# Expert routing in three groups of token tiles instead of two, with two of the three sigmoids moved into the state-space loop

## The reference

```python
x = x + _L1_attn_ref(_L1_cond_ref(x, ...), ...)        # state-space model
x = x + _L1_ffn_ref(_L1_cond2_ref(x, ...), ...)        # gate, then experts

def _L1_ffn_ref(hidden_states, w_gate, w1, w2, w3):
    x = hidden_states.reshape(-1, D)
    router_logits = x @ w_gate.T
    routing_weights = jax.nn.softmax(router_logits.astype(jnp.float32), axis=-1)
    routing_weights, selected_experts = jax.lax.top_k(routing_weights, TOP_K)
    routing_weights = routing_weights / jnp.sum(routing_weights, axis=-1, keepdims=True)
    out = jnp.zeros_like(x)
    for e in range(NUM_EXPERTS):
        expert_weight = jnp.sum(routing_weights * (selected_experts == e), axis=-1, keepdims=True)
        h = jax.nn.silu(x @ w1[e].T) * (x @ w3[e].T)
        out = out + h @ w2[e].T * expert_weight
    return out.reshape(B, S, D)
```

## Time and profile before

| what | value |
| --- | --- |
| median of three executions (lowest, highest) | 700.4 us (700.04, 701.31) |
| span of the profiled execution, first to last instruction | 698.6 us |
| busy PE, PEld, DVE, ACT, POOL | 537.6, 392.4, 405.1, 370.2, 147.6 us |
| chain that ended last, by engine | PE 52%, DVE 31%, ACT 9%, issue 4%, DMA 2% |
| mean granted clock of TensorE | 0.910 of full speed |
| weight fetches of the experts | 23 x 1408 KB and 23 x 768 KB |

### The profile page before, as it was taken

How to read it: one execution, slowest core, us unless ns; L and a number is a source line. 1 busy time by engine, 2 the same in 40 slices (tenths; PEclk the granted TensorE clock), 3 DMA queues, 4 the chain that set the end, 5 groups by cost and what they waited for, 6 DMA issues and landing times.

```text
span 698.6 us, 13906 instructions
## 1 busy us (share of the span) xinstructions
PE 537.6 (77%) x5666; PEld 392.4 (56%) x5668; DVE 405.1 (58%) x597; ACT 370.2 (53%) x791; POOL 147.6 (21%) x115
## 2 busy tenths in 40 slices
PE   0095778677587855579998999979539999999980
PEld 0053555555455722454655666648529999997570
DVE  5889999989996578946835445543541111211223
ACT  6986789968877238645566455562312222222212
POOL 1000000000001138702068455220021222222210
PEclk9997699998878999899999999998659999999996
DMA  9500000000001000000000000000159999988825
GB/s 351 180 1 1 1 1 1 2 1 1 1 1 32 1 0 1 2 0 1 2 3 2 3 2 2 2 2 3 61 206 421 421 419 354 335 332 314 327 110 188
DMA packets 18479, 71.38 MB, mean 102 GB/s; under 512 B 4848, under 2 KB 9968, under 8 KB 14704
## 3 DMA queue, kind: packets, MB, share of 16 engines
q1 hardware_dynamic: 15408, 64.20, 24.2%
q0 software_dynamic: 1920, 5.25, 2.0%
q10 hardware_dynamic: 1088, 1.05, 0.4%
HBM read 65.77 MB, written 4.72 MB: 101 GB/s over the span
## 4 chain that ended last, share of the span: by engine, by line
PE 52%; DVE 31%; ACT 9%; issue 4%; DMA 2%; POOL 1%; SPq 0%; ACTq 0%; DVEq 0%; POOLq 0%
PE PS L1412 40%; DVE arena L933 4%; DVE nmx L1020 4%; DVE arena L930 4%; PE PS L1918 2%; PE PS L1987 2%; PE PS L1694 1%; DVE arena L945 1%; DVE arena L944 1%; DVE R L947 1%; DVE A L952 1%; DVE arena L939 1%; DVE arena L940 1%; PE PS L1559 1%; ACT arena L767 1%
## 5 line engine op out<-in xcount | busy, mean ns | idle before, releaser
L1412 PE MATMUL PS<-arena 128*128 128x128 f32 (+5 forms) x1374 | 156.6, 295 | 17.7 <-DVE arena L1117 11.6
L1412 PEld LDWEIGHTS PS<-arena 128*128 128x128 f32 (+4 forms) x1376 | 125.7, 164 | 41.1 <-issue 24.5
L611 ACT ACTIVATE arena<-PS,nmx 128x128 f32<-128x128 f32 (+1 forms) x128 | 52.2, 423 | 34.7 <-DVE nmx L1020 34.7
L1360 DVE TENSOR_TENSOR R<-arena,PS 128x128 f32<-128x128 f32 x16 | 4.6, 288 | 88.8 <-ACT arena L861 88.8
L1476 PE MATMUL PS<-arena 32*128 32x128 f32 (+1 forms) x128 | 22.9, 439 | 34.0 <-ACT arena L611 33.8
L389 POOL TENSOR_SCALAR arena<-ident,gcol 128x128 f32<-128x128 f32 x4 | 2.4, 605 | 220.2 <-DMA gcol<-in_gcol 220.2
L449 POOL TENSOR_TENSOR arena<-arena 128x1024 f32<-128x1024 f32 x16 | 37.8, 2369 | 42.9 <-DVE arena L1199 34.8
L481 POOL DMA_INDIRECT ypair<-arena,oid x20 | 19.8, 988 | 122.1 <-ACT arena L867 122.1
L1412 PE MATMUL PS<-arena,R 128*128 128x256 f32 x192 | 44.2, 380 | 0.6 <-ACT arena L867 0.6
L1412 PEld LDWEIGHTS PS<-arena,R 128*128 128x128 f32 x192 | 35.2, 190 | 5.1 <-issue 1.0
L933 DVE TENSOR_TENSOR_SCAN arena<-dmat,arena 128x1023 f32<-128x1023 f32 x16 | 37.6, 2348 | 0.6
(11 more groups left out here) (302 smaller groups left out, 1205.3 us busy)
## 6 DMA issues: line engine op xcount, KB each, us to landing
arena<-in_moe SPq DMA_DIRECT2D x23, 1408.0 KB, 7.8
arena<-in_moe SPq DMA_DIRECT2D x23, 768.0 KB, 9.6
inproj<-in_inproj SPq DMA_DIRECT2D x1, 1344.0 KB, 10.5
arena<-in_fT SPq DMA_DIRECT2D x1, 1024.0 KB, 5.0
xT<-in_xT SPq DMA_DIRECT2D x1, 1024.0 KB, 5.4
R<-in_w1T SPq DMA_DIRECT2D x1, 1024.0 KB, 7.5
R<-in_w2T SPq DMA_DIRECT2D x1, 1024.0 KB, 9.5
R<-in_w3T SPq DMA_DIRECT2D x1, 1024.0 KB, 11.6
```

The source lines that it names most:

```text
L611: sc.activation(pr[u % 2][:, j, 0:n], PS[:, 2 * (u % 2) + j // 2, (j % 2) * 256:(j % 2) * 256 + n], ACT.Exp, bias=nmx[:, u % 2, j:j + 1], ...
L1412: last = mm(dst, l, r, start=(n == 0), stop=(n == len(pairs) - 1))
```

## The change

The eight tiles are routed in groups of four, two and two (`ROUTE`), with PSUM banks 0, 1 and 3 for a group's logits and ranks. The sigmoid of group 0 moves from behind `inverse_root(5)` to ahead of it, the sigmoid of group 1 is new in ScalarE's iteration 7, ahead of `turned(6)`, and the sigmoid of group 2 stands after the loop, now ahead of the first copy of token rows. VectorE and TensorE take the groups in the order 1, 0, 2.

```diff
 ROUTE = ((0, 4), (4, 6), (6, 8))          # new; ROUTE_BANK = (0, 1, 3)
@@ ScalarE
+            def sigmoid_tiles(g):
+                lo, hi = ROUTE[g]
+                act.wait_ge(S["dve_x"], X_FFN + hi)
+                sc.activation(A[:, :, lo * P:hi * P], xT[:, :, lo * P:hi * P], ACT.Sigmoid).then_inc(S["act_sg"], 1)
...
                 if i + 1 < NT:
                     by_chunk(i + 1)
+                else:
+                    sigmoid_tiles(1)
+                    sc.preload_act_table_set(LN_EXP)
                 if i:
                     turned(i - 1)
+                    if i == NT - 2:
+                        sigmoid_tiles(0)
+                        sc.preload_act_table_set(LN_EXP)
                     inverse_root(i - 1)
-                if i == NT - 2:
-                    sigmoid_x(3, 0)
-                    sc.preload_act_table_set(LN_EXP)
...
+            sigmoid_tiles(2)
             token_rows(0)
-            sigmoid_x(3, 1)
             token_rows(1)
@@ VectorE
-            gate(3, 0)
+            gate_tiles(0)
+            gate_tiles(1)
             gated(NT - 1)
             add_out(NT - 2)
...
+            top_values(1)
+            top_two(1)
             top_values(0)
             top_two(0)
             add_out(NT - 1)
-            gate(3, 1)
-            top_values(1)
-            top_two(1)
             places(0)
+            gate_tiles(2)
+            place_rows(0)
+            places(1)
+            top_values(2)
+            top_two(2)
+            place_rows(1)
             blocks()
-            places(1)
+            places(2)
+            place_rows(2)
             tokens_of_blocks()
@@ TensorE
+            logits(1)
+            turn(NT - 1)
             logits(0)
-            turn(NT - 1)
+            output(NT - 1)
             token_rows(0)
-            output(NT - 1)
             ranks(0)
-            logits(1)
-            pe.wait_ge(S["dve_x"], X_SSD)
+            ranks(1)
+            logits(2)
             token_rows(1)
-            ranks(1)
+            ranks(2)
             pe.wait_ge(S["act_atok"], 1)
             token_x(0)
```

More of the change, by code:

```diff
@@ L830, in _ @@
             token_x(1)
-            act.wait_ge(S["dve_mask"], 2)
+            act.wait_ge(S["dve_mask"], 3)
             sc.activation(wt[:, 0, :], delta[:], ACT.Sigmoid)
@@ L1251, in _, with gate_tiles, top_values, top_two @@
                     front(i + 1)
-            gate(3, 0)
+            def gate_tiles(g):
+                lo, hi = ROUTE[g]
+                dve.wait_ge(S["act_sg"], 7 + g)
+                a_ = A[:, :, lo * P:hi * P]
+                r_ = R[:, 3, lo // 4].rearrange("p (a n) -> p a n", a=CT)[:, :, lo % 4 * P:((hi - 1) % 4 + 1) * P]
+                done(v.tensor_tensor(a_, a_, r_, ALU.mult), "dve_A")
+            gate_tiles(0)
+            gate_tiles(1)
             gated(NT - 1)
             add_out(NT - 2)
[L1256 to L1263, removed]
+            def top_values(g):
+                lo, hi = ROUTE[g]
+                dve.wait_ge(S["pe_lg"], (6, 2, 8)[g])
+                done(v.tensor_copy(lg[:, lo:hi, :], PS[:, ROUTE_BANK[g], NE * lo:NE * hi].rearrange("p (i e) -> p i e", e=NE)))
+                for i in range(lo, hi):
                     done(v.max(top[:, i, :], lg[:, i, :]))
-            def top_two(c):
-                h = slice(4 * c, 4 * c + 4)
-                for i in range(4 * c, 4 * c + 4):
+            def top_two(g):
+                lo, hi = ROUTE[g]
+                h, b48 = slice(lo, hi), [P, hi - lo, NE]
+                for i in range(lo, hi):
                     done(v.max_index(tix[:, i, :], top[:, i, :], lg[:, i, :]))
@@ L1276, in top_two, with places @@
                 done(v.tensor_tensor(mb[:, h, :], oh[:, 0, h, :], oh[:, 1, h, :], ALU.add), "dve_mask")
-            def places(c):
-                h = slice(4 * c, 4 * c + 4)
+            def places(g):
+                lo, hi = ROUTE[g]
+                h = slice(lo, hi)
                 dve.wait_ge(ld["route"], 7 * 16)
-                dve.wait_ge(S["pe_rank"], 2 * c + 1)
+                dve.wait_ge(S["pe_rank"], (1, 2, 4)[g])
                 for s in range(2):
-                    done(v.tensor_tensor(pick[:, s, h, :], bank(c, 4 * NE).rearrange("p (i e) -> p i e", i=4), oh[:, s, h, :], ALU.mult))
+                    done(v.tensor_tensor(pick[:, s, h, :], PS[:, ROUTE_BANK[g], NE * lo:NE * hi].rearrange("p (i e) -> p i e", e=NE), oh[:, s, h, :],
+                                         ALU.mult))
                 done(v.tensor_reduce(rnk[:, :, h], pick[:, :, h, :], X, ALU.add))
@@ L1288, in places, with place_rows @@
                 done(v.scalar_tensor_tensor(pos[:, :, h], quo[:, :, h], -float(UNIT), rnk[:, :, h], ALU.mult, ALU.add))
-                four = [P, 4, UNIT]
+            def place_rows(g):
+                lo, hi = ROUTE[g]
+                h, some = slice(lo, hi), [P, hi - lo, UNIT]
                 for s in range(2):
-                    done(v.tensor_tensor(posoh[:, s, h, :], iop[:].unsqueeze(1).broadcast_to(four),
-                                         pos[:, s, h].unsqueeze(2).broadcast_to(four), ALU.is_equal))
+                    done(v.tensor_tensor(posoh[:, s, h, :], iop[:].unsqueeze(1).broadcast_to(some),
+                                         pos[:, s, h].unsqueeze(2).broadcast_to(some), ALU.is_equal))
             def blocks():
                 full, odd = fullodd[:, 0, :], fullodd[:, 1, :]
-                dve.wait_ge(S["pe_rank"], 2)
+                dve.wait_ge(S["pe_rank"], 3)
                 done(v.tensor_scalar(nunit[:], bank(2, NE), 1.0 / UNIT, 31.5 / UNIT, ALU.mult, ALU.add))
@@ L1831, in _, with logits @@
                     output(i - 1)
[L1834 to L1837, removed]
+            def logits(g):
+                pe.wait_ge(S["dve_A"], 7 + g)
+                for i in range(*ROUTE[g]):
+                    acc(PS[:, ROUTE_BANK[g], i * NE:(i + 1) * NE], [(A[:, kt, i * P:(i + 1) * P], wgate[:, kt, :]) for kt in range(CT)], "pe_lg")
             def token_rows(c):
@@ L1845, in token_rows, with ranks @@
                 last.then_inc(S["pe_at"], 1)
-            def ranks(c):
-                pe.wait_ge(S["dve_mask"], c + 1)
-                if c:
+            def ranks(g):
+                pe.wait_ge(S["dve_mask"], (2, 2, 3)[g])
+                if g == 2:
                     acc(bank(2, NE), [(oneb[:], mb[:, k, :]) for k in range(NT)], "pe_rank")
[L1852 to L1855, removed]
+                for i in range(*ROUTE[g]):
+                    for k in range(i + 1):
+                        last = mm(PS[:, ROUTE_BANK[g], i * NE:(i + 1) * NE], ub[:] if k == i else oneb[:], mb[:, k, :], start=(k == 0), stop=(k == i))
                 last.then_inc(S["pe_rank"], 1)
@@ L2013 @@
 ROWS_BANK = (2, 5)
+ROUTE = ((0, 4), (4, 6), (6, 8))
+ROUTE_BANK = (0, 1, 3)
 X_ATT = NT
```

## The result

| | before | after |
| --- | --- | --- |
| median of the timed executions, 4 each (lowest, highest) | 700.39 us (700.04, 701.31) | 689.66 us (689.18, 691.69) |
| span of the profiled execution | 698.6 us | 687.9 us |
| mean granted clock of TensorE | 0.910 | 0.905 |

The change makes the kernel faster: ratio 0.986, 95% interval 0.9839 to 0.9882. Forecast were 689.4 us, and 11.0 us of gain in the span; it is 10.7.

The account below looks back on a forecast made before the run. Routing bounds when the fixed 90 us expert stage starts: 4.9 us earlier at the last addition, plus VectorE's 18.55 us instead of 24.62 to `gid`, give 11.0 us: span 687.6, with 1.8 timed offset 689.4 us, range 687.0 to 692.6.

Parts of the forecast that it names:

- A: First sigmoid moves into ScalarE's gap in iteration 6: TensorE's 2.97 us wait goes, tile 7's VectorE work starts 5.76 us earlier.
- B: Second sigmoid queued ahead of tile 6's transposes: TensorE waits about 0.7 us for `turned(6)`; tile 6's addition ends at 479.35.
- C: Routing of tiles 4, 5 and 0 to 3 before the last addition, which ends at 485.7, 4.9 us earlier.
- D: After the last addition: VectorE's remaining routing up to the end of `gid` takes 18.55 us, against 24.62.
- two-tile shapes: Unknown lengths of VectorE's two-tile routing instructions: together 2.4 us less or 2.6 more than taken.
- the cover: Last two tiles' logits (1.9 us) run beside `place_rows(0)` and `places(1)` (2.17 us); price 1.9 us if lost.
- the first weights: Expert weights issued near 496.8 land by 504.5, before the first expert matmul wants them at about 509.
- 5.85 - 3.06 = 2.79 more: Tile 7's state, in-chunk products and transposes on TensorE shorten from 5.85 to 3.06 us at full clock.
- 1 (half clock stays): Small waits left on TensorE still lower the clock and tile 7 runs at half: price 2.79, 692.2 us; chance 0.10.
- 2 (a table switch costs more than its row): Two ScalarE table switches outlast their loads, 1.5 us more each, so tile 7's state copy is late: 695.1 us; chance 0.03.
- 3 (the experts start colder): Expert stage starts on a colder TensorE and full clock returns late; two half-clock steps cost 15.8 us: 705.2; chance 0.04.
- 4 (the gather does not follow `gid`): Something other than `gid` releases the experts' gather and keeps its time, so nothing moves: 700.4 us; chance 0.03.

Follow-up runs that it names:

- e1: Kernel before, with only the first sigmoid and its two table loads moved ahead of `inverse_root(5)`, routing still in two groups: 696.52 us, ratio 0.9963.
- e2: Changed kernel with the first group's sigmoid put back behind `inverse_root(5)`, three groups kept: 694.48 us, ratio 0.9932.
- e5: Changed kernel plus 26 tiny unread matmuls behind the condition's matmul, where TensorE is idle: 688.27 us, ratio 0.9825.
- e6: Changed kernel plus 64 tiny unread matmuls behind the condition's matmul, 256 instructions in all: 691.51 us, ratio 0.9873.
- e8: Kernel before plus 26 tiny unread matmuls behind the condition's matmul: 697.69 us, ratio 0.9958.
- e3: Changed kernel plus 26 small unread fp32 matmuls at TensorE's start, ahead of the condition's matmul: 699.3 us, ratio 0.9992.
- e7: Changed kernel plus 26 tiny unread matmuls behind the condition's, and `place_rows` on GpSimd instead of VectorE: 686.76 us, ratio 0.98.
- e4: Changed kernel with `place_rows` (one-hot rows of a token's place) on GpSimd instead of VectorE: 690.4 us, ratio 0.9876.

## Why the prediction was right

The stretch from tile 7's first state matmul to `gid` can be cut at two rows, the transposes that follow tile 7's scores on TensorE (`turn(6)`) and the addition of tile 7 on VectorE (its first instruction, L1237 before and L1246 after). Each column is a difference of two starts in one trace, so it is free of what happens ahead of it; A, B with C, and D are the forecast's terms.

| kernel | state to transposes (A) | transposes to addition (B, C) | addition to `gid` (D) | sum |
| --- | --- | --- | --- | --- |
| before | 11.00 | 12.34 | 25.31 | 48.65 |
| forecast | 5.24 | 13.1 | 19.26 | 37.6 |
| after | 7.10 | 12.37 | 19.22 | 38.69 |
| e1, the move alone | 7.09 | 12.34 | 25.31 | 44.74 |
| e2, the move undone | 11.73 | 12.39 | 19.25 | 43.37 |
| e5, without the stop | 5.26 | 13.11 | 19.21 | 37.58 |
| e6, the stop back | 7.09 | 12.38 | 19.20 | 38.67 |
| e8, before without its stop | 9.83 | 12.34 | 25.28 | 47.45 |

- **D was right to 0.1 us.** 18.52 measured for 18.55. The two-tile shapes, taken between half a four-tile round and a whole one, came out near the value taken, and the cover held: the last logits (488.41, at half speed or near it) delay nobody, and neither do the stores nor the first weights. What the forecast had not followed are the second step's weights, for which TensorE waits 0.87 us. The last addition ends at 486.32 instead of 485.7; that lateness comes from A.
- **A: the mechanism was right, the size was not.** The wait is gone, the clock stays at 1.00 (the two windows above), and ScalarE's work fits the gap as worked out. Of 5.76 us, 3.90 came. The step that failed is the term "5.85 - 3.06 = 2.79 more", by which tile 7 goes as fast as the tile before it once the clock stays up: it left out that TensorE can run out of instructions. The scores of both tiles hold an edge of a block, but TensorE comes to tile 6's 5 us after its packet's start and to tile 7's 0.8 us after. e5 takes only the stop away and has 5.74 of the 5.76. Before's own trace shows such a stop, 1.79 us at 383.64 in the same line's matmuls; at half clock TensorE came to tile 7's edge 2.6 us after the packet's start, and the scores had no stop.
- **B and C were right, and hid part of A's miss.** The forecast let TensorE wait 0.7 us for `turned(6)`, and so give 0.8 of A back. With the stop TensorE is late itself: ScalarE's sigmoid is done, and the 0.8 isn't paid (12.37 instead of 13.1). In e3, e5 and e7, where the stop is gone, that wait is there, 0.67 us. So the stop cost 1.86 in the first column and 1.1 in the sum.
- **The sum.** 38.69 against 37.6: 1.1 of the 11.0 did not come. 0.48 of it was made up because the loop's last tiles start that much earlier in this execution (457.96 for 458.44 in the earlier trace rows); no work of the change lies ahead of that, and the stops at tile 1 differ between the traces (1.05 and 1.79 us). The last 0.3 came behind the gather, where the first 44 expert matmuls took 6.56 us instead of 7.18, of which the second step's wait took half back (0.87 us where a pause of 0.57 was before). Neither was forecast: that the time came within 0.3 us of 689.4 is in part luck.
- **The rivals.** 1 (half clock stays): no, by the same two windows. 2 (a table switch costs more than its row): no; from the first load's start to the inverse root, 463.05 to 466.72, it is 3.67 us for rows of 3.62. The Trainium skill, "ScalarE: Activation LUTs", section "What ACT_TABLE_LOAD costs", adds a drain of about 1380 ns to each switch; the trace does not agree, for nothing of it is in these 3.67 us. 3 (the experts start colder): no; the first step begins at half clock as before, its 44 matmuls took 6.56 us in after and 6.80 to 7.88 in e1, e2, e4, e5 and e7, and the second runs in 5.2; a swing of one microsecond, not the 11 it would have needed. 4 (the gather does not follow `gid`): no, 505.70 - 504.65 is 1.05 as it was.

The two parts add up: the move alone has 3.9 in the sum and the routing alone 5.3, together 9.2 of the 9.96 that both have. The missing 0.8 is, but for some hundredths, e2's first column (11.73 for 11.00): its stop stands behind its wait, where before had only the wait.

**What stays open.** Why the clock falls behind one stop and not behind another: in before it fell behind 1.79 us at tile 1, while the same stop of 1.05 to 1.60 us in after, e1, e2, e4 and e6 had no fall behind it, nor had the 1.63 in after, and in e4 it fell 8 us behind a stop of 1.63, with TensorE busy in between. And why the same work behind the same wait takes 1.2 us longer at half clock in one trace than in another (before and e8). These move the time by a microsecond or two from one execution to the next, and a gain below that isn't told from a single trace.

## What to carry to other kernels

When a change takes a wait off an engine, look at what that engine will run into at its new speed, its own instruction supply among it: a row of some hundred short instructions with an "issue" stop near its end, anywhere in the trace, is a warning for every like row. Whether it strikes there depends on where the block's edge falls and how long its packet has been on the way. Cut a stretch at two or three rows that stay in every version and compare the pieces, since the sum of two errors can look right (here a miss of 1.9 us showed as 1.1). And a sum of VectorE's rows, gap included, holds to a tenth of a microsecond where nothing else is late.

## What the runs showed of the hardware

- TensorE's program comes in blocks of 256 instructions, one packet of 16 KB each. A shift by 104 instructions moved a stop of 1.63 us away and one by 256 put it back on the same matmul. No edge of a block was passed less than 2.18 us after the start of its packet, and the stops ended 2.18 to 2.74 us after it. So an edge cost nothing where TensorE came to it later than that, and 1.05 to 1.79 us behind 119 to 122 of 128 matmuls of some 10 ns. To add idle instructions anywhere ahead moves such stops: e5 and e6 differ in their number alone, by 1.1 us in the sums above. Their medians lie 3.2 us apart, and the rest of that is not explained.
- 26 tiny matmuls with a load of 32 columns took 3.45 us (with the condition's), as many with 128 columns 11.68 (busy time of TensorE in 5:25 of e3), both at clock 1.00; the loads fill 3.34 and 11.59 us of it, so here the load's width sets the pace.
- GpSimd compares 128x64 with a scalar in 0.45 us (16 such took 7.2 us in e7), where VectorE does eight of them in 0.88 (two instructions of 128x256): it pays only where GpSimd is idle and the result isn't needed at once.
